# Fixed pads, shared sums stored without the residual, and a router woven into the shared experts, in a two-layer attention and mixture-of-experts kernel

## The chip, the cores and the metric

The kernel runs on one core of a Trainium2 chip. The metric is the device time of one execution in microseconds. Before the change it is 3535.88 us, the median of three runs (3523.08 to 3542.6).

## What is computed

The reference runs two layers over x, 4 sequences of 1024 tokens of width 256. A layer is an attention block and a feed-forward block, each behind a layer norm and each added to x:

```python
x = x + attn(_layernorm(x), ...)      # 16 heads of 16, causal
x = x + ffn(_layernorm(x), ...)
def ffn(x):
    shared_out = sum(relu(x @ sw1 + sb1) @ sw2 + sb2, 2 experts) / 2
    probs = softmax(x @ router_w + router_b)          # 32 experts
    topk_p, topk_i = top_k(probs, 6)                  # gates, normalised
    routed_out = sum over the experts e of gate[:, e] * (relu(x @ rw1[e] + rb1[e]) @ rw2[e] + rb2[e])
    return shared_out + routed_out
```

The first layer's attention has a distance penalty in its scores, the second's has not; both use the same feed-forward weights. Everything is float32; products are made from a high part and a rest (three matmuls for one).

## The kernel before, in words

Each engine has its own program, written out by hand, and the engines meet at semaphores. A layer has five phases, and `phase_end` between them is a barrier: every engine drains, adds to `s_phase` and waits until all five have done so.

- Phase 0 makes q, k and v for all tokens.
- Phase 1 is attention, in 16 units (`NU`) of four heads of one sequence. The router's work on a batch (a sequence) that has been through attention is spread over the four units after it (`route_step`): merge and output projection (`merge_batch`), layer norm of the rows (`normalise_rows`), their transposes and high and rest parts (`router_input`, which SP then stores to `xT_scratch` with `store_xT`), `logits`, `select` (the six largest), `place_rows` (a row number in `expert_rows` for each token and expert). POOL then scatters the rows to their experts: `dispatch(b)` is 48 indirect DMAs of 128 rows of 1280 bytes. In phase 1 this is done for batches 0, 1 and 2. Batch 2's `select` and `place_rows` come in the very last unit.
- Phase 2 is the same router chain for batch 3 (the last, `B - 1`), and after it the shared experts over 8 blocks (`NBLK`) of 512 tokens. A block is three chunks (`NCS`): `hidden` (PE, six matmuls of 512 columns) into PSUM, relu on ACT, `hidden_split` on DVE, `summed` (PE, six more), then a copy on ACT (`copy_out`), transposes back (`transpose_shared`) and on DVE `out_add`, which adds the block to the rows of x that SP loaded from `expert_sum0` into `xs32`; SP stores it back there. SP also loads the blocks' inputs (`load_shared_xT`, 1 MB each into two buffers), and the routed experts' raw weights `w2raw` and `w1raw`, which phase 3 needs. Between two blocks SP runs `close_regions` for four experts: it reads the end of an expert's rows from `prow` and writes 384 pad rows (480 KB, DRAM to DRAM) behind them, with `L545`. `expert_rows` has a fixed region for each of the 32 experts, so that a tile that runs past the expert's last row finds pads.
- Phase 3 runs the routed experts over 96 tiles of 384 rows. A table made in phase 2 (`tile_table`) gives each tile its expert and its first row. Results are added to `expert_sum0` and `expert_sum1` in turn by indirect DMA. `expert_sum1` was filled with zeros (4 MB) at the start of phase 1.
- Phase 4 adds the two sums into x.

SP's queue of DMAs is in order: what it issues later lies behind what it issued before on the same rings, and a wait of SP holds up all that is written behind it. POOL has a queue of its own.

Of the kernel before, what the change touches and what calls it, by code (L numbers as in the profile page):

```python
# [20 lines left out]
F32 = mybir.dt.float32  # L21
# [39 lines left out]
EARLY = 11  # L61
# [100 lines left out]
def build(nc, a, out):  # L162
# [6 lines left out]
    acc = [nc.dram_tensor(f"expert_sum{i}", (NTOK + TT, D), F32, kind="Internal").ap() for i in range(2)]  # L169
    tabd = nc.dram_tensor("tile_table_scratch", (P, 2), U32, kind="Internal").ap()  # L170
# [4 lines left out]
    with ctx:  # L175
# [38 lines left out]
        rowb = x[:, 4096:6656].rearrange("p (r t w) -> p r t w", r=2, t=TPB)  # L214
# [9 lines left out]
        posu = x[:, 7672:7736].bitcast(U32)  # L224
# [18 lines left out]
        table = work[:, 4032:5069]  # L243
        lincl, thr, tau, tau_rows = (table[:, i:j] for _, i, j in columns(TABLE))
        tmp = work[:, 5072:6096]
        xs32 = work[:, 6144:8192].rearrange("p (r t) -> p r t", r=2)
        raw = work[:, 8192:9728].rearrange("p (r n) -> p r n", r=3)
        ysb = work[:, 9728:10752].rearrange("p (f t) -> p f t", f=KD)
        hbuf = work[:, 10752:12288].rearrange("p (r t) -> p r t", r=3)
# [21 lines left out]
        cnt, m_e, c_e, st_e, le_e, in_e = (osb[:, NE * i:NE * i + NE] for i in range(6))  # L271
        tabf = osb[:, 192:194]
# [4 lines left out]
        tab2, prow = route_u[:, 0:2], route_u[:, 2:2 + NE]  # L277
# [33 lines left out]
        s_raw = [sem(f"shared_raw_loaded{r}") for r in range(3)]  # L311
# [7 lines left out]
        s_pad, s_zb, s_tc = sem("pad_rows_stored"), sem("second_sum_cleared"), sem("table_constants_loaded")  # L319
        s_xsl = [sem(f"shared_xT_loaded{r}") for r in range(2)]  # L320
        s_ysl = [sem(f"shared_x_loaded{r}") for r in range(2)]
        s_yss = [sem(f"shared_x_stored{r}") for r in range(2)]
# [38 lines left out]
        def _(sp):  # L361
# [9 lines left out]
            sp.dma_start(w2d, a["w2r"]).then_inc(s_init, 16)  # L371
            sp.dma_start(rows[0:TT], a["pads"]).then_inc(s_init, 16)
# [4 lines left out]
            with sp.Fori(0, NL) as L:  # L377
# [87 lines left out]

                load_values(0, 0)
# [6 lines left out]
                for u in range(NU):  # L473
# [76 lines left out]
                for blk in range(2):  # L550
                    load_shared_xT(blk)
# [1308 lines left out]
```

## Time and profile before

| | |
|---|---|
| median of three runs | 3535.88 us (3523.08 to 3542.6) |
| the profiled execution, its own time | 3527.31 us |
| span in its profile | 3525.2 us |
| PE busy | 2749.4 us, 78% |
| DVE busy | 2095.4 us, 59% |
| ACT busy, POOL busy | 1516.8 us, 1506.2 us |
| DMA | 540.23 MB, mean 153 GB/s |
| mean granted TensorE clock | 0.893 |

The span runs from the first to the last instruction; the execution's own time is 2.1 us longer. Busy time counts no waits. The shares are means over phases of very different kinds, so the stretches around phase 2 are read apart. PE is the matmul engine, DVE the vector engine, ACT the scalar engine, POOL the engine that issues indirect DMAs, SP the one that issues plain ones.

### The profile page before, as it was taken

To read this page: it belongs to the slowest core of one execution; us is meant where nothing else is said; L and a number is where in the kernel's file an instruction comes from. 1 tells how busy PE (TensorE), PEld (TensorE's weight loads), DVE (VectorE), ACT (ScalarE), POOL (GpSimd) and SP (SyncE) were. 2 spreads that over 40 slices of the span, in tenths; PEclk is the share of its full clock that TensorE was granted. 3 is DMA by queue.
4 is the path that set the end of the run, shared out by engine and by line. 5 is a ranking of instruction groups with operands and counts; after the bars stand their busy time and mean duration, and the time that the engine had idled before them with its cause. 6 is when DMAs were issued, how large, how long until landed. Compare 5 with 4: busy or idle time off the path is not lost. (4 is left out here: it accounts for less than half of the span.)

```text
span 3525.2 us, 67642 instructions
## 1 busy us (share of the span) xinstructions
PE 2749.4 (78%) x17576; PEld 2050.3 (58%) x17576; DVE 2095.4 (59%) x4312; ACT 1516.8 (43%) x2406; POOL 1506.2 (43%) x1118
## 2 busy tenths in 40 slices
PE   4789999998255999888285999999953669899880
PEld 3555555554144888787263555555522558888770
DVE  5665677764242767666375666767623337766662
ACT  2244444444011666666241454444430126666660
POOL 1520005050450688888445000222232518888882
PEclk9899999999577999999687999999975779999995
DMA  7974445451587788888668734555327768888886
GB/s 240 254 146 82 72 83 155 82 156 52 187 292 259 150 157 154 151 150 150 145 204 174 160 66 74 115 122 113 100 82 227 281 224 156 152 150 147 150 146 167
DMA packets 329916, 540.23 MB, mean 153 GB/s; under 512 B 49690, under 2 KB 246172, under 8 KB 324444
## 3 DMA queue, kind: packets, MB, share of 16 engines
q1 hardware_dynamic: 228332, 399.18, 43.2%
q0 software_dynamic: 101376, 138.47, 22.3%
q8 instruction: 106, 1.74, 0.2%
q14 instruction: 102, 0.84, 0.1%
HBM read 301.60 MB, written 283.67 MB: 166 GB/s over the span
## 5 line engine op out<-in xcount | busy, mean ns | idle before, releaser
L1390 POOL DMA_INDIRECT expert_sum<-x,route_u x576 | 950.4, 1650 | 218.4 <-issue 125.0
L1357 POOL DMA_INDIRECT expert_rows<-x x384 | 375.4, 978 | 1304.6 <-DVE x L928 1190.0
L1206 ACT ACTIVATE work<-ps 128x1024 f32<-128x1024 f32 (+3 forms) x768 | 593.9, 810 | 726.1 <-PE ps L1490 529.9
L774 DVE TENSOR_REDUCE small<-ps 128x1 f32<-128x512 f32 (+3 forms) x1216 | 726.9, 656 | 207.6 <-PE ps L1476 141.0
L1472 PE MATMUL ps<-split 128*128 128x512 f32 (+3 forms) x1536 | 512.4, 410 | 81.5 <-SPq L355 43.7
L1762 PE MATMUL ps<-split 97*128 97x256 f32 x3456 | 466.8, 291 | 86.2 <-ACT x L1287 85.6
L1486 PE MATMUL ps<-split 128*128 128x512 f32 (+3 forms) x1536 | 499.7, 405 | 18.6 <-DMA split<-split 17.6
L1762 PEld LDWEIGHTS ps<-split 97*128 97x128 f32 x3456 | 447.2, 197 | 114.8 <-issue 111.9
L1744 PE MATMUL ps<-split 128*88 128x384 f32 x2304 | 456.0, 347 | 0.4 <-DVE split L1089 0.2
L1472 PEld LDWEIGHTS ps<-split 128*128 128x128 f32 x1536 | 278.3, 202 | 274.4 <-DVE small L774 141.2
L1744 PEld LDWEIGHTS ps<-split 128*88 128x88 f32 x2304 | 352.6, 157 | 40.9 <-issue 0.8
L1287 ACT ACTIVATE x<-ps,osb 128x256 f32<-128x256 f32 x576 | 231.6, 471 | 300.3 <-DMA expert_sum<-x,route_u 292.8
L1486 PEld LDWEIGHTS ps<-split 128*128 128x128 f32 x1536 | 299.6, 201 | 77.9 <-ACT work L1206 42.4
L1503 PE MATMUL ps<-work,split 128*32 128x512 f32 (+3 forms) x3072 | 328.4, 503 | 0.0
L1109 DVE TENSOR_TENSOR split<-x,split 88x768 fp32r<-88x768 f32 x192 | 183.1, 954 | 101.2 <-ACT split L1274 99.4
L1490 PE MATMUL ps<-maskk,identb 128*128 128x128 bf16 x1024 | 233.2, 235 | 0.0
L1269 ACT ACTIVATE x<-ps,osb 88x384 f32<-88x384 f32 x384 | 209.8, 583 | 42.7 <-PE ps L1744 39.3
L1732 PE MATMUL ps<-ident,x 128*128 128x128 f32 x1152 | 168.5, 285 | 70.8 <-DMA osb<-in_b1r 39.1
L1089 DVE TENSOR_TENSOR split<-ps,split 128x768 fp32r<-128x768 f32 x192 | 182.9, 952 | 49.7 <-ACT split L1258 49.5
L1476 PE MATMUL ps<-maskq,identb 128*128 128x128 bf16 (+2 forms) x704 | 188.6, 268 | 0.0
L1258 ACT ACTIVATE split<-ps 128x768 fp32r<-128x768 f32 x192 | 157.2, 819 | 68.6 <-PE ps L1732 68.4
L1732 PEld LDWEIGHTS ps<-ident,x 128*128 128x128 f32 x1152 | 134.9, 147 | 85.0 <-issue 84.0
(170 smaller groups left out, 2926.6 us busy)
## 6 DMA issues: line engine op xcount, KB each, us to landing
x<-expert_rows SPq DMA_DIRECT2D x192, 480.0 KB
split<-qks_scratch SPq DMA_DIRECT2D x192, 256.0 KB
qks_scratch<-split SPq DMA_DIRECT2D x64, 512.0 KB, 4.5
expert_rows<-in_pads SPq DMA_DIRECT2D x65, 480.0 KB, 5.2
v_scratch<-work SPq DMA_DIRECT2D x64, 256.0 KB, 4.3
split<-v_scratch SPq DMA_DIRECT2D x32, 512.0 KB, 14.2
xT_scratch<-split SPq DMA_DIRECT2D x16, 1024.0 KB, 13.9
split<-xT_scratch SPq DMA_DIRECT2D x16, 1024.0 KB, 8.5
```

The lines of the kernel that those rows point to most:

```text
L774: v.tensor_reduce(cols[:, heads[0]:heads[0] + len(heads), i], ps[:, task_bank(n), 0:w * len(heads)].rearrange("p (h k) -> p h k", k=w), AX ...
L1206: c.activation(pexp[:, (s % 2) * 2 + h, :, BLK - w:], ps[:, 2 * h:2 * h + 2, BLK - w:], ACT.Exp).then_inc(s_pe, 1)
L1287: c.activation(ye[:, r3, k, :], ps[:, 4 + k, 0:D], ACT.Copy, scale=gsel[:, j, k:k + 1]).then_inc(s_tev, 1)
L1357: pool.indirect_dma_start(rows, bass.IndirectOffsetOnAxis(ap=posu[:, t * 8 + k:t * 8 + k + 1], axis=0), rowb[:, t // TPB, t % TPB, :], Non ...
L1390: pool.indirect_dma_start(acc[r], bass.IndirectOffsetOnAxis(ap=idx[:, j, k:k + 1], axis=0), ye[:, r3, k, :], None, compute_op=ALU.add).the ...
L1472: last = mm(bank[:, e, :], stack[:, r, 0, h, i * P:i * P + P], stack[:, r, 1, h, first:first + w], start=e == 0, stop=not diagonal and e = ...
L1486: last = mm(ps[:, h, BLK - w:], stack[:, r, 1, h, kb * P:kb * P + P], stack[:, r, 0, h, (qt + 1) * BLK - w:(qt + 1) * BLK], start=True, st ...
L1490: last = mm(ps[:, h, BLK - w:BLK - w + P], identb[:, :], maskk[:, :], start=False, stop=True, skip_group_check=True)
L1503: last = mm(ps[32 * h:32 * h + 32, 6, BLK - w:], vreg[:, r, kb, h, :], pexp[:, (s % 2) * 2 + h // 2, h % 2, BLK - w:], start=kb == 0, stop ...
L1732: last = tr(ps[:, k, n * P:n * P + P], xrow[:, r3, n, k * P:k * P + P], ident[:, :])
L1744: last = mm(ps[0:HC, 2 + c, 0:TT], w1e[:, r, ws, k * HID + c * HC:k * HID + c * HC + HC], xe[:, r, xp, k * TT:k * TT + TT], start=e == 0 a ...
L1762: last = mm(ps[:, 4 + n, 0:D], he[0:HB, r, xp, c * TT + n * P:c * TT + n * P + P], w2e[0:HB, r3, ws, c * D:c * D + D], start=e == 0 and c ...
```

## The change

It has five parts.

1. Pads. The 384 pad rows of an expert lie in front of its rows, at a fixed address. SP writes them during phase 1, two experts in each unit. Rows start 384 further on (`base`), and the tiles of an expert are counted back from the end of its rows (`rend`), so its last tile reaches into the pads. `close_regions`, which needed the counts, is gone.
2. Shared sums. `out_copy` writes a block's result without the rows of x, and SP stores it to `expert_sum1`. The filling with zeros and the loads into `xs32` are gone; the residual stays in `expert_sum0`.
3. Shared weights come as one load from a copy in DRAM that is made at the start of the kernel (0.79 MB), in the last unit of phase 1, into the place of a stack that is free by then. Their high parts (DVE) and rests (POOL) are made in that unit too. 13 experts of `w2raw`, 10 of `w1raw` and the inputs of blocks 0 and 1 are loaded in phase 1; the other 19 of `w2raw` and 22 of `w1raw` stay in phase 2, those of `w1raw` behind the last scatter (7) and the last stores (15).
4. In phase 2 the router chain of batch 3 and the shared experts are woven into each other on PE, DVE and ACT: block 0's hidden products first, then merge, and so on.
5. `dispatch(B - 2)` moves from phase 1 to phase 2, ahead of `dispatch(B - 1)`, which has its own `rowb` and `posu` buffers.

```diff
+            sp.dma_start(wsd, a["wsh"]).then_inc(s_init, 16)
...
                     if u == 0:
-                        sp.wait_ge(s_init, 64)
-                        sp.dma_start(acc[1][0:NTOK].rearrange("(t p) d -> p t d", p=P),
-                                     a["zeros"].unsqueeze(1).broadcast_to([P, NT, D])).then_inc(s_zb, 16)
+                        sp.wait_ge(s_init, 80)
                         sp.wait_ge(s_bod, (L + 1) * NT)
                         sp.dma_start(xd.rearrange("(t p) d -> p t d", p=P), xv).then_inc(s_xst, 16)
+                    for e in range(2 * u, 2 * u + 2):
+                        sp.dma_start(rows[REG0 + e * STRIDE:REG0 + e * STRIDE + TT], a["pads"]).then_inc(s_pad, 16)
...
+                    if u == 12:
+                        load_w1(0, EARLY)
+                sp.wait_ge(s_pv, (L * NU + NU - 3) * NS + NS + 2)
+                apart(sp)
+                sp.dma_start(raw.rearrange("p r n -> p (r n)"), wsd).then_inc(s_raw, 16)
                 sp.dma_start(b1, a["b1"]).then_inc(s_shared, 16)
+                load_w2(16, 24)
+                load_w2(27, 32)
...
-                for blk in range(NBLK):
-                    close_regions(4 * blk, 4 * blk + 4)
-                    if blk < NBLK - 2:
-                        load_shared_xT(blk + 2)
-                    store_shared_x(blk)
-                    if blk < NBLK - 2:
-                        load_shared_x(blk + 2)
-                load_w1(EARLY, NE)
+                for blk in range(4, NBLK):
+                    store_shared(blk)
+                load_w2(24, 27)
                 for r in range(2):
                     sp.wait_ge(s_disp[r], (L + 1) * (NBLK // 2 * TPB * TOPK * 16))
                     apart(sp)
+                load_w1(EARLY, 17)
+                for r in range(2):
                     sp.wait_ge(s_yss[r], (L + 1) * (NBLK // 2 * 16))
                     apart(sp)
+                load_w1(17, NE)
...
-                for b in range(B - 1):
+                for b in range(B - 2):
                     dispatch(b)
-                phase_end(pool, L, 1)
...
+                phase_end(pool, L, 1)
+
+
+                dispatch(B - 2)
                 dispatch(B - 1)
...
+                for c in range(NCS):
+                    hidden(0, c)
+                for r in range(2):
+                    merge_transpose(B - 1, r)
...
+                shared_part(0, 0)
+                shared_part(0, 1)
+                router_input(B - 1, 0)
+                shared_part(0, 2)
+                logits(B - 1, 0)
+                router_input(B - 1, 1)
+                shared_part(1, 0)
+                logits(B - 1, 1)
+                shared_part(1, 1)
+                shared_part(1, 2)
+                ranks(B - 1)
+                shared_part(2, 0)
...
                 merge_batch(B - 1)
                 for c in range(NCS):
-                    weights_hi(c)
-                dve.wait_ge(s_shared, (L + 1) * 16)
-                v.tensor_scalar(b1h, b1, 1.0 / NSH, None, ALU.mult).then_inc(s_b1h, 1)
+                    hidden_split(0, c)
                 batch_scales(B - 1)
                 for r in range(2):
                     normalise_rows(B - 1, r)
-                    router_input(B - 1, r)
-                    logits(B - 1, r)
+                router_input(B - 1, 0)
+                shared_step(0)
+                logits(B - 1, 0)
+                router_input(B - 1, 1)
+                logits(B - 1, 1)
                 shift_logits(B - 1)
+                out_copy(0, 0)
                 select(B - 1)
+                for c in range(NCS):
+                    hidden_split(2, c)
+                out_copy(0, 1)
                 place_rows(B - 1)
```

`shared_part(k, c)` on PE is `hidden(k + 1, c)`, `summed(k, c)` and, for c < 2, `transpose_shared(k - 1, c)`; `shared_step(k)` on DVE is `hidden_split(k + 1, c)` and `out_copy(k - 1, c)`.

On POOL, before, batch 2's 48 scatters stand ahead of the barrier that ends phase 1 (L356):

```order
L1357 DMA expert_rows<-x 144512x320 x48
L356 ISA
L1367 ISA
L1368 TENSOR_TENSOR split<-work,split 128x2x128
L1370 TENSOR_TENSOR split<-work,split 128x256
```

With the change, the rests of the shared weights stand there, and both late batches' scatters follow the barrier (L358):

```order
L1381 TENSOR_TENSOR split<-split 128x256
L358 ISA
L1367 REGISTER_ALU
L1371 DMA expert_rows<-x 144512x320 x48
L1371 DMA expert_rows<-work,x 144512x320 x48
L358 ISA
```

48 scatters have moved from before the barrier to behind it. On PE, before, phase 2 begins behind the barrier (L356) with the merge of batch 3 (L1535 transposes, L1548 products):

```order
L356 REGISTER_ALU
L1529 REGISTER_ALU
L1463 REGISTER_ALU
L1535 MATMUL ps<-ident,work 128x128 x4
L1463 REGISTER_ALU
L1535 MATMUL ps<-ident,work 128x128 x8
L1463 REGISTER_ALU
L1535 MATMUL ps<-ident,work 128x128 x4
L1542 REGISTER_ALU
L1548 MATMUL ps<-x 128x256 x4
```

With the change it begins with block 0's hidden products (L1674), and the same merge (now L1550) comes behind them:

```order
L1709 ISA
L1709 REGISTER_ALU x2
L1669 REGISTER_ALU
L1670 ISA
L1674 MATMUL ps<-split 128x512 x6
L1670 REGISTER_ALU
L1674 MATMUL ps<-split 128x512 x6
L1670 REGISTER_ALU
L1674 MATMUL ps<-split 128x512 x6
L1544 REGISTER_ALU
L1478 REGISTER_ALU
L1550 MATMUL ps<-ident,work 128x128 x4
```

18 matmuls have moved ahead of the router chain. On SP, before, the first rows of phase 2 behind the table's load are two block inputs, then a part of w2 (from `w2_scratch`), the residual rows' store (L459) and loads (L524), and the store of the transposed rows (L464):

```order
L510 DMA work<-in_table 128x1037
L548 ISA
L517 DMA split<-xT_scratch 128x2048 x2
L539 DMA split<-w_scratch 112x8x512
L455 REGISTER_ALU
L459 DMA expert_sum<-x 128x4x256 x2
L554 REGISTER_ALU
L524 DMA work<-expert_sum 128x4x256 x2
L539 DMA split<-w_scratch 112x8x512
L462 REGISTER_ALU
L464 DMA xT_scratch<-split 128x2048
```

With the change two parts of w2 (L474) come first, then the input of block 2 (L482), the residual's store (L462), block 3's input and only then the transposed rows' store (L467), behind a wait for block 1's products:

```order
L537 DMA work<-in_table 128x1037
L474 DMA split<-w_scratch 112x8x512 x2
L480 ISA
L482 DMA split<-xT_scratch 128x2048
L458 REGISTER_ALU
L462 DMA expert_sum<-x 128x4x256 x2
L480 ISA
L482 DMA split<-xT_scratch 128x2048
L465 REGISTER_ALU
L467 DMA xT_scratch<-split 128x2048
```

The loads of the residual are gone, and the store of the transposed rows has two more megabyte loads ahead of it.

## Rows read from the trace of the kernel before

**Rows 1.** The page's groups: line, engine, operation, busy us, mean ns, idle before
```profile
L1357 POOL DMA_INDIRECT expert_rows<-x x384 | 375.4, 978 | 1304.6 <-DVE x L928 1190.0
```
**Rows 2.** Windows: start:end, length, busy of each engine, clock, DMA share, GB/s
```profile
core 0: us, PE busy (x) PEld busy (x) DVE busy (x) ACT busy (x) POOL busy (x), PEclk, DMA share, GB/s
867.20:934.70 67.50, 0.00 (x0) 0.00 (x0) 3.21 (x19) 0.00 (x0) 46.10 (x48) 0.52 0.32 117
934.70:1147.60 212.90, 117.40 (x475) 96.31 (x475) 75.66 (x190) 28.99 (x44) 56.84 (x56) 0.72 0.83 278
2669.00:2882.90 213.90, 116.98 (x474) 95.60 (x474) 75.86 (x190) 28.99 (x44) 56.93 (x56) 0.72 0.83 276
```
**Rows 3.** Timeline of POOL, layer 1: start, us, what [idle before <- released by]
```profile
870.21 0.95 POOL L1357 DMA_INDIRECT expert_rows<-x  x1 [104.30 <-DVE x L928]
...
929.66 0.96 POOL L1357 DMA_INDIRECT expert_rows<-x  x1 [0.30 <-issue]
...
993.52 0.98 POOL L1357 DMA_INDIRECT expert_rows<-x  x1 [38.72 <-DVE x L928]
...
1055.45 0.96 POOL L1357 DMA_INDIRECT expert_rows<-x  x1 [0.30 <-issue]
```
**Rows 4.** Timeline of PE around phase 2, layer 1, and layer 2's start
```profile
935.10 3.65 PE L1535 MATMUL ps<-ident,work 128*128 128x128 f32 x16 [67.93 <-POOLq L355]
...
994.40 7.03 PE L1674 MATMUL ps<-split 128*128 128x512 f32 x18 [0.45 <-issue]
...
1020.16 2.90 PE L1674 MATMUL ps<-split 128*128 128x512 f32 x6 [8.30 <-DMA split<-xT_scratch]
...
1026.18 1.52 PE L1685 MATMUL ps<-split 128*128 128x512 f32 x6
1027.54 1.53 PE L1674 MATMUL ps<-split 128*128 128x512 f32 x6
...
1040.26 2.90 PE L1674 MATMUL ps<-split 128*128 128x512 f32 x6 [8.93 <-DMA split<-xT_scratch]
...
1147.59 1.51 PE L1732 MATMUL ps<-ident,x 128*128 128x128 f32 x6 [19.68 <-DMA osb<-in_b1r]
...
2669.36 3.55 PE L1535 MATMUL ps<-ident,work 128*128 128x128 f32 x16 [68.28 <-POOLq L355]
```
**Rows 5.** Timeline of SP in phase 2, layer 1: DMA issues
```profile
961.40 0.34 SPq L464 DMA_DIRECT2D xT_scratch<-split  x1
...
1124.47 5.50 SPq L545 DMA_DIRECT2D expert_rows<-in_pads  x4
...
1130.76 0.50 SPq L535 DMA_DIRECT2D work<-in_w1r  x1
```
**Rows 6.** Timeline of DVE, end of phase 1 and in phase 2, layer 1
```profile
855.13 0.26 DVE L799 RECIPROCAL small<-ps 128x16 f32<-128x16 f32 x1 [11.51 <-PE ps L1513]
...
870.52 0.42 DVE L802 TENSOR_TENSOR work<-ps,small 128x256 f32<-128x256 f32 x1
...
972.25 0.69 DVE L856 CAST split<-ps 128x512 fp32r<-128x512 f32 x1 [3.90 <-DMA xT_scratch<-split]
...
1024.01 0.43 DVE L1019 CAST split<-work 128x512 fp32r<-128x512 f32 x1 [11.42 <-ACT work L1241]
1024.48 0.69 DVE L1021 TENSOR_TENSOR split<-work,split 128x512 fp32r<-128x512 f32 x1
```
**Rows 7.** Timeline of PE, first units of phase 1: layer 1, layer 2
```profile
273.33 0.79 PE L1486 MATMUL ps<-split 128*128 128x512 f32 x1 [4.49 <-DMA split<-split]
...
2008.92 0.50 PE L1486 MATMUL ps<-split 128*128 128x512 f32 x1 [3.06 <-DMA split<-split]
```
**Rows 8.** DMA issues by line: count, KB each, median us from issue to landing
```profile
expert_rows<-in_pads SPq DMA_DIRECT2D x65, 480.0 KB, 5.2
...
split<-xT_scratch SPq DMA_DIRECT2D x16, 1024.0 KB, 8.5
...
expert_sum<-work SPq DMA_DIRECT2D x16, 512.0 KB, 6.1
...
w_scratch<-in_w2r SPq DMA_DIRECT2D x1, 26.5
```

More of the change, by code:

```diff
@@ L60 @@
 W2ROWS = 112
-EARLY = 11
+EARLY = 10
 UPB = T // BLK
@@ L310, in build @@
                                    sem("selection_counted"))
-        s_raw = [sem(f"shared_raw_loaded{r}") for r in range(3)]
+        s_raw = sem("shared_raw_loaded")
         s_wh, s_wl = sem("shared_hi_done"), sem("shared_lo_done")
@@ L538, in load_w2 @@
-                def load_w2(first, last):
-                    sp.dma_start(w2raw[:, first * W2:last * W2].rearrange("p (e n) -> p e n", n=W2),
-                                 w2d[first:last].rearrange("e p n -> p e n")).then_inc(s_wr2, 16)
-                def close_regions(first, last):
-                    with sp.Fori(first, last) as e:
-                        at = sp.value_load(prow[0:1, ds(e, 1)], min_val=REG0, max_val=NROWS - TT)
-                        sp.dma_start(rows[ds(at, TT), :], a["pads"]).then_inc(s_pad, 16)
+                    if u == 12:
+                        load_w1(0, EARLY)
@@ L1699, in transpose_shared, with shared_part @@
                     last.then_inc(s_yt, 1)
-                def shared_block(blk):
-                    for c in range(NCS):
-                        hidden(blk, c)
-                        if blk and c == 2:
-                            transpose_shared(blk - 1, 0)
-                        if c >= 2:
-                            summed(blk, c - 2)
-                        elif blk:
-                            summed(blk - 1, c + 1)
-                        if blk and c == 2:
-                            transpose_shared(blk - 1, 1)
+                def shared_part(k, c):
+                    if k < NBLK - 1:
+                        hidden(k + 1, c)
+                    summed(k, c)
+                    if k and c < 2:
+                        transpose_shared(k - 1, c)
                 for c in range(NCS):
                     pe.wait_ge(s_wl, L * NCS + c + 1)
-                for blk in range(NBLK):
-                    shared_block(blk)
+                for c in range(NCS):
+                    hidden(0, c)
+                for r in range(2):
+                    merge_transpose(B - 1, r)
+                for r in range(2):
+                    for h in range(2):
+                        merge_product(B - 1, r, h)
+                shared_part(0, 0)
[10 more added lines that the diff above has]
+                shared_part(2, 0)
+                pe.wait_ge(s_ms, (L + 1) * B)
+                task_free(route_task(B - 1, 15))
+                apart(pe)
+                mm(ps[:, task_bank(route_task(B - 1, 15)), 0:NE], oneb[:, :], msumb, start=True,
+                   stop=True).then_inc(s_mj, 1)
                 for c in (1, 2):
-                    summed(NBLK - 1, c)
+                    shared_part(2, c)
+                for k in range(3, NBLK):
+                    for c in range(NCS):
+                        shared_part(k, c)
                 for f in range(2):
```

230 lines of the change are left out of this document (114 added, 116 removed).

## The prediction

> **What bounds the kernel now.** I read the page's groups first, then the windows of the stretches in which PE idles, then the timelines of POOL, PE, SP and DVE there. The page shows that POOL's scatters of rows (384 in two layers, mean 978 ns) have little idle time between them once they run: what they cost is decided by when they may start [rows 1]. The windows show two bad stretches in each layer. Between 867.20 and 934.70 PE does nothing at all and POOL is the only engine with work [rows 2]: the reader is to see that batch 2's scatters begin at 870.21, when DVE has just placed the rows, that the last begins at 929.66, and that PE's next matmul at 935.10 waited 67.93 us for POOL's share of the barrier [rows 3, 4]. Layer 2 has the same, 68.28 us [rows 4]. The second stretch is phase 2, from there to phase 3's first transpose at 1147.59, 212.5 us. PE is busy 117.4 of the window's 212.9 at a granted clock of 0.72 (a mix of the levels 1.2 and 2.4 GHz), while the DMA engines are busy 83% at 278 GB/s [rows 2, 4]. In it the router chain of batch 3 comes first, alone, until its first scatter at 993.52; then the shared blocks, which begin 20.1 us apart (1020.16, 1040.26), each behind an 8 to 9 us wait for its input [rows 3, 4]. POOL is done with the last scatter at 1056.4; it is not the bound of phase 2, SP's queue is: four pads (1.97 MB) stand ahead of each block's input, and the last four hold SP from 1124.47 to 1130 and the loading of w1 behind them, for which phase 3 waits [rows 3, 5].
>
> **Batch 2's scatters out of phase 1.** DVE's last work in phase 1 ends at 870.52 + 0.42 = 870.9 [rows 6]. From the last scatter's end (930.6) to PE's first matmul (935.1) the barrier takes 4.5 us, with POOL's queue just emptied; without that I take 2 (bounds 0.5 and 4.5). So phase 2 starts at 873 and not at 935.1: 62 us a layer (60 to 64). What comes into the last unit instead is hidden: DVE's six casts of the shared weights stand where it idled 11.5 us before 855.13 [rows 6], and POOL's rests lie beside the attention. If the load they need were late, all of it would come back; it is issued one unit ahead, so I charge nothing (up to 3).
>
> **Phase 2, counted from its first matmul.** The new order [the two lists of PE] makes one chain, then a scatter, then a tail.
> - *Until batch 3's rows are placed.* Before it takes 993.52 - 935.10 = 58.4 us [rows 3, 4]. Put into it are 18 hidden products at the head, 7.0 us at the low clock as at 994.40 [rows 4], and on DVE three blocks' splits, 9 pairs of 1.16 us (0.47 to the second instruction, then 0.69), 10.4 us [rows 4, 6]. The weight casts leave. PE's other products fall largely beside DVE's work, and with PE busy the router's own matmuls should run nearer the full clock: the first six products after a wait take 2.90 us, those in a run 1.53 [rows 4]. The store of the transposed rows, for which DVE already waits 3.9 us at 972.25 [rows 6], now has a block's input ahead of it (8.5 us [rows 8]); I charge 5. Sum 58.4 + 7 + 10.4 + 5 = 80.8, less some 10 for the overlap and the clock: 70 (bounds 60 and 90).
> - *Scatters.* Batch 2's need 870.21 to 930.6, 60.4 us, alone; batch 3's needed 993.52 to 1056.4, 62.9 us, beside DVE [rows 3]. The queue is free at 62, rows are there at 70, the last scatter ends at 133 and has landed at 135.
> - *PE.* At 70 blocks 0 and 1 and part of 2 are done. A block at full clock is six groups of six products, 1.36 us from one to the next (1026.18 to 1027.54 [rows 4]), with transposes about 9.2 us; five and a half more give 50, a stall of 5 for the count of rows, the last copies 3, so 128, and the last store lands 6.1 us later [rows 8] at 134. POOL and PE end together: either is cover for the other, and if one is late the phase is.
> - *Tail.* w1 is issued when both have landed, at 135. Before, 21 experts' load of 3.7 MB from 1130.76 released phase 3 at 1147.59, 16.8 us later, with pads and a store still ahead in the queue [rows 4, 5]. Now 22 experts without them: 17. Phase 3 begins at 152 instead of 212.5: 60.5 us a layer.
>
> **DMA.** The window moved 278 GB/s x 212.9 us = 59.2 MB [rows 2]. Out go 32 pads (15.7 MB, 480 KB each [rows 8]), the residual's loads (4.2), 13 experts of w2 (3.0), two block inputs (2.1), 1.8 of w1 and 0.8 of raw weights; in come 48 scatters of 128 x 1280 bytes (7.9). That leaves 39.5 MB, 260 GB/s over 152 us, below the 278 that the stretch held at a share of 83%. At 278 it would need 142 us. So the queue isn't the bound, but not far from it; that is my reason for 5 us on the store above.
>
> A rule speaks against the new scatters. The row: beside DVE's work 48 scatters took 62.9 us, alone 60.4, so DVE costs them 2.5 us, with some ten split pairs inside [rows 3]. The Trainium skill (SBUF — State Buffer, the part on the engine ports and the trap in which DVE blocks DMA) says that a float32 copy on DVE locks GpSimd, which writes the descriptors, out of the shared port for the whole instruction. By the rule in full all 24 pairs would be added to the scatters, as the second rival has it, and the execution would take 3339. By the row it is 2.4 times 2.5 us over both batches, 6 us, of which only batch 3's share is on the path. I go by the row.
>
> **Phase 1 and the start.** Two pads a unit are 0.98 MB, issued early in the unit; they are through long before the next rows of maxima. The zeros' 4 MB are gone from the first unit, where PE waited 4.49 us (273.33) and 3.06 us (2008.92) for its rows of maxima behind them [rows 7]: -5 of the 7.6. At the start of the kernel the copy of the shared weights (0.79 MB) joins a queue in which the 3.67 MB of w2 take 26.5 us [rows 8] and in front of the first weights: 26.5 x 0.79 / 3.67 = 5.7 at most, +4. Phases 3 and 4 have the same tiles and additions: nothing.
>
> **Sum** against the profiled execution's own time: 3527.3 - 2 x (62 + 60.5) - 5 + 4 = 3281. That execution is 8.6 us under the median of 3535.9; half of that is added: 3285.
>
> **The rivals.**
> - *Phase 2 stays bound by DMA* (0.14). For it: 83% busy now, a second batch's scatters come in, and six block inputs still wait for a buffer. Against it: the pads, ahead of every input, are gone. If each block from 70 on shows its input's whole 8.5 us [rows 8] beside its 9.2 of matmuls, six take 106, so 176, the store lands at 182, phase 3 begins at 199: 13.5 saved there instead of 60.5, 3285 + 94 = 3379.
> - *The scatters starve beside DVE*, the lock above as this kernel would have it (0.07): 24 pairs x (0.43 + 0.69) us [rows 6] = 27 us a layer on POOL's chain. For it: 2.5 us show. Against it: only these. 3285 + 54 = 3339. The rule is the Trainium skill's, named above.
> - *The wait has only moved* (0.02): batch 2's 60.4 us push batch 3's scatters and with them the end by as much; no gain from that part, and 3536 if phase 2's own gain goes with it. Against it: 91 us pass between the last scatter's end and phase 3's first transpose, and batch 3's rows aren't placed before 58.4 anyway [rows 3, 4].
> - *Slower* (0.03): pads ahead of the rows of maxima. Each unit but the first of a layer starts when these 16 KB have landed, and they use the pads' queue. If a pair of pads (5.2 us each [rows 8]) lay ahead each time, 30 units x 10.4 = 312 us are lost against 246 gained: 3600. It decides from 8.2 us a unit. The pads are issued right behind a unit's load, the rows late in the next, so I expect both to be through by then; the two waits of [rows 7] show the mechanism, with 8 MB ahead.
>
> The forecast itself has 0.74, with a range of its own of 3250 to 3325: rows placed at 60, where POOL's queue is the bound (127 instead of 135 for the landing), and all of the zeros' wait back, give 3285 - 16 - 3 = 3266; a barrier of 0.5 us and a head of 4 instead of 7 make it 3255; rows at 90 give 3285 + 40 = 3325. The range for 8 in 10 takes in the starving scatters: 3245 to 3340. A measurement can tell 0.5% (18 us) from no change: faster 0.96, same 0.01, slower 0.03.
>
> **What the profile after would show.** PE's idle time in front of phase 2 is 6 us, not 68. Batch 2's scatters start within 3 us of the barrier, batch 3's about 70 us after it; 48 take 61 to 64. Shared blocks from the third on begin 9 to 11 us apart, with waits for inputs under 2 us. Phase 3's first transpose comes 145 to 160 us after phase 2's first matmul. The wait of 4.49 us in phase 1 is gone, and the first weights' split is 2 to 6 us later. It would be wrong if blocks still wait 5 us or more for their input, if batch 3's rows come at 90 or later, or if waits for the rows of maxima appear in the units of phase 1.

## The result and the profile after

In the text TensorE, VectorE or DVE, ScalarE, GpSimd and SyncE are the engines that the rows call PE, DVE, ACT, POOL and SP.

The changed kernel took 3251.9 us (median of 4 runs, 3248.9 to 3254.4), the kernel before 3539.2 beside it on the same chip; the ratio is 0.9196 with a 95% interval of 0.9165 to 0.9226. On a second chip it was 3245.5 us and 0.9200 (0.9178 to 0.9221). The forecast was 3285, with a range of 3245 to 3340. The profiled execution took 3251.45 us, 275.9 less than the profiled one of before; the sum had it at 3281. The time lies in the range, 33 us under the forecast and 7 us above the range's lower end; on the second chip it is above that end by 0.5 us.

TensorE's rows at the same places as in [rows 4], from the timeline after:

```profile
877.69 2.90 PE L1674 MATMUL ps<-split 128*128 128x512 f32 x6 [4.54 <-DVEq L357]
...
941.71 0.19 PE L1732 MATMUL ps<-x,oneb 128*128 128x32 bf16 x1 [2.79 <-DVE x L931]
...
961.66 1.52 PE L1674 MATMUL ps<-split 128*128 128x512 f32 x6
...
970.79 1.52 PE L1674 MATMUL ps<-split 128*128 128x512 f32 x6
...
979.91 1.52 PE L1674 MATMUL ps<-split 128*128 128x512 f32 x6
...
996.82 0.63 PE L1697 MATMUL ps<-ident,work 128*128 128x128 f32 x4 [0.88 <-DVE work L1034]
...
1020.47 1.51 PE L1752 MATMUL ps<-ident,x 128*128 128x128 f32 x6 [23.02 <-DMA osb<-in_b1r]
...
2471.69 6.98 PE L1674 MATMUL ps<-split 128*128 128x512 f32 x18 [4.54 <-DVEq L357]
...
2613.30 1.51 PE L1752 MATMUL ps<-ident,x 128*128 128x128 f32 x6 [23.54 <-DMA osb<-in_b1r]
```

Ahead of phase 2 TensorE idles 4.54 us instead of 67.93 and 68.28. Phase 2, from the first matmul to phase 3's first transpose, is 142.8 us in layer 1 and 141.6 in layer 2, where it was 212.5 and 213.6. The late blocks start 9.1 us apart, and no wait for `xT_scratch` is left among them. The row at 941.71 is the product that counts each expert's rows; TensorE waited 2.79 us for it. Its last transposes of the shared blocks end 119.8 us into the phase, and the last copy of a sum on DVE 120.5 us into it.

GpSimd's scatters (as [rows 3]) and SyncE's last issues (as [rows 5]), same layer:

```profile
877.91 0.98 POOL L1371 DMA_INDIRECT expert_rows<-x  x1 [10.98 <-DVEq L357]
...
941.46 0.95 POOL L1371 DMA_INDIRECT expert_rows<-work,x  x1 [1.62 <-DVE work L921]
...
1002.23 0.96 POOL L1371 DMA_INDIRECT expert_rows<-work,x  x1 [0.30 <-issue]
```
```profile
983.29 15.34 SPq L545 DMA_DIRECT2D expert_sum<-work  x4
998.68 0.57 SPq L474 DMA_DIRECT2D split<-w_scratch  x1
1006.30 0.98 SPq L470 DMA_DIRECT2D work<-in_w1r  x2
```

Batch 2's 48 scatters begin right behind the barrier and batch 3's follow with a gap of 1.62 us. The last ends at 1003.2, 125.5 us into the phase; SyncE issues w1 at 1006.3, when it has landed, and phase 3 follows 14.2 us later. So the chain that sets the end of phase 2 is now GpSimd's two runs of scatters, the second of which begins when batch 3's rows are placed; TensorE ends 6 us before it. The router's one long wait on DVE in the phase, to be read against 972.25 in [rows 6], is for the store of the transposed rows, 6.26 us:

```profile
918.37 0.69 DVE L849 CAST split<-ps 128x512 fp32r<-128x512 f32 x1 [6.26 <-DMA xT_scratch<-split]
```

The windows of the phase, to be read against [rows 2]:

```profile
core 0: us, PE busy (x) PEld busy (x) DVE busy (x) ACT busy (x) POOL busy (x), PEclk, DMA share, GB/s
877.69:1020.47 142.78, 103.87 (x474) 84.74 (x475) 70.08 (x183) 28.77 (x44) 99.05 (x98) 0.83 0.81 275
2471.69:2613.30 141.61, 102.42 (x475) 83.66 (x475) 70.62 (x183) 28.80 (x44) 99.83 (x98) 0.84 0.82 276
```

TensorE's same work takes 14 us less there, at a granted clock of 0.83 instead of 0.72. By stage the 275.9 us go: the start and layer 1's phase 0 +3.5, its phase 1 and the barrier -60.9, its phase 2 -69.7, its phases 3 and 4 -5.0; then layer 2 in the same order +1.2, -66.8, -72.0 and -6.2.

### The profile page after: what moved, and what is told of

The parts are those of the page before. It is cut to its first block and busy times, and to the rows that moved or that the text cites. A ratio compares the mean times of both kernels' runs of the same rounds, so it can differ in the third digit from the quotient of the medians.

```text
span 3249.4 us, 67087 instructions
## 1 busy us (share of the span) xinstructions
PE 2719.4 (84%) x17576; PEld 2022.0 (62%) x17576; DVE 2096.4 (65%) x4312; ACT 1517.0 (47%) x2406; POOL 1497.5 (46%) x1118
## 5 line engine op out<-in xcount | busy, mean ns | idle before, releaser
L1405 POOL DMA_INDIRECT expert_sum<-x,route_u x576 | 940.1, 1632 | 213.3 <-issue 119.4
L1371 POOL DMA_INDIRECT expert_rows<-x x288 | 280.7, 975 | 1010.0 <-DVE x L921 902.3
## 6 DMA issues: line engine op xcount, KB each, us to landing
split<-v_scratch SPq DMA_DIRECT2D x32, 512.0 KB, 14.2
```

The costliest lines, as they stand in the source:

```text
L1371: pool.indirect_dma_start(rows, bass.IndirectOffsetOnAxis(ap=posu[b][:, t * 8 + k:t * 8 + k + 1], axis=0), rowb[b][:, t // TPB, t % TPB, : ...
L1405: pool.indirect_dma_start(acc[r], bass.IndirectOffsetOnAxis(ap=idx[:, j, k:k + 1], axis=0), ye[:, r3, k, :], None, compute_op=ALU.add).the ...
```

## The experiments

Each ran beside the kernel before on the same chip; "phase 2" is layer 1's and layer 2's length from its first matmul to phase 3's first transpose, read from TensorE's timeline of the profiled execution. It is not the same twice: the eight phases of kernels whose code for it is the changed kernel's (this one, its repetition and the two below that only change phase 1) are 139.0 to 143.7 us long.

**One part undone: batch 2's scatters early again.**

```diff
+                dispatch(B - 2)
                 phase_end(pool, L, 1)
-                dispatch(B - 2)
                 dispatch(B - 1)
```


> The changed kernel with one part undone: batch 2's 48 scatters are issued before the barrier that ends phase 1, as in the kernel before. Theory (POOL's chain bounds both places): TensorE again stands idle 64 to 68 us ahead of phase 2 (4.5 in the changed kernel), and phase 2 stays close to its 142 us, since batch 3's scatters begin at row placing (about 62 us into it) anyway: 3252 + 2 x 63 = about 3378 (3370 to 3390). Rival (the late scatters slowed phase 2, by POOL and DVE sharing a port or by DMA traffic): phase 2 falls to 130 to 136 us, and the time is 3352 to 3366.

3372.5 us, ratio 0.9558 (0.9525 to 0.9591). The idle time is back, and the phase is nearly unchanged, 139.3 and 139.8 us, though 48 scatters fewer run in it:

```profile
938.32 2.04 PE L1674 MATMUL ps<-split 128*128 128x512 f32 x4 [68.20 <-POOLq L357]
...
1077.61 1.51 PE L1752 MATMUL ps<-ident,x 128*128 128x128 f32 x6 [23.74 <-DMA osb<-in_b1r]
```
```profile
938.32:1077.61 139.29, 101.47 (x475) 83.04 (x475) 69.36 (x183) 28.80 (x44) 51.51 (x50) 0.84 0.71 225
```

The theory holds. The moved scatters gain 63 us a layer. What they cost in phase 2, 2 to 4 us against the changed kernel's profile, is inside the spread of 139.0 to 143.7, so no cost is shown. DMA carries 225 GB/s here and 275 in the changed kernel, for nearly the same length, so the bytes don't set that length.

**The kernel before with late scatters alone.** `dispatch(B - 2)` behind the barrier, batch 3's rows in `work[:, 1440:4000]`, early w1 only for 4 experts:

```diff
-EARLY = 11
+EARLY = 4
-                for b in range(B - 1):
+                for b in range(B - 2):
                     dispatch(b)
                 phase_end(pool, L, 1)
 ...
+                dispatch(B - 2)
                 dispatch(B - 1)
```


> The kernel before with one part of the change alone: batch 2's scatters after the barrier (with rows of their own for batch 3, in room taken from the early w1 loads, so 28 instead of 21 experts' w1 are loaded behind the last scatter). Theory (phase 2 of the kernel before, 212 us, is bound by SP's queue of pads and block inputs, so 62 us more of POOL's scatters fit beside it): TensorE's 68 us idle ahead of phase 2 falls to 4 to 6, phase 2 stays at 212 to 220: 3535 - 2 x 60 = about 3415 (3405 to 3430). Rival (DMA-bound phase 2): the moved scatters' traffic lengthens phase 2 by 15 to 60 us, and the time is 3440 to 3535.

3410.9 us, 0.968 (0.9639 to 0.9722), as the theory has it. The idle time fell to 4.31 and 4.22 us, phase 2 grew to 222.8 and 222.3, 2 to 3 us more than the theory's 220. Of these 9 to 10 us some 3 are the longer load of w1 behind the last scatter (TensorE's last wait is 22.65 us, [rows 4] has 19.68). Another 5 to 6 are longer waits for the blocks' inputs, of which this is the first: 46.2 and 46.5 us in the two layers, 41.2 and 40.3 before.

```profile
872.88 3.65 PE L1538 MATMUL ps<-ident,work 128*128 128x128 f32 x16 [4.31 <-DVEq L356]
...
962.92 2.90 PE L1677 MATMUL ps<-split 128*128 128x512 f32 x6 [8.60 <-DMA split<-xT_scratch]
```

The DMA engines moved 301 GB/s in this phase 2, so the 278 of [rows 2] were not the most that they can do there.

**The kernel before with fixed pads in phase 1 alone.** Cut to SyncE's lines:

```diff
+                    for e in range(2 * u, 2 * u + 2):
+                        sp.dma_start(rows[REG0 + e * STRIDE:REG0 + e * STRIDE + TT], a["pads"]).then_inc(s_pad, 16)
 ...
-                    close_regions(4 * blk, 4 * blk + 4)
```


> The kernel before with one part of the change alone: pads fixed in front of each expert's rows, stored in phase 1 (two per unit). Theory (the pads in SP's queue made phase 2 212 us): without them the queue ends early, POOL's 48 scatters of batch 3 end at 58 + 63 = 121 us or TensorE's blocks after the router chain at 130 to 140, and phase 3 begins 145 to 160 us after phase 2's first matmul: -55 to -67 us a layer, 3400 to 3430; the 68 us idle ahead of phase 2 stays. Rival (residual loads, stores and scatters hold it as much): phase 2 stays over 180 us, and the time is over 3470. If the 5 to 6 us of phases 3 and 4 come from pads in front, they show here too.

3443.4 us, 0.9749 (0.9704 to 0.9795), between the two. Phase 2 fell to 169.8 and 170.0, 43 us less and not 55 to 67. Its scatters end 123.8 us into the phase, but the shared blocks, which start only behind the router chain, go on until 154:

```profile
1007.26 0.98 POOL L1359 DMA_INDIRECT expert_rows<-x  x1 [40.89 <-DVE x L930]
```
```profile
1008.14 6.30 PE L1676 MATMUL ps<-split 128*128 128x512 f32 x18 [0.45 <-issue]
...
1099.10 0.63 PE L1699 MATMUL ps<-ident,work 128*128 128x128 f32 x4 [0.88 <-DVE work L1031]
...
1115.86 1.51 PE L1734 MATMUL ps<-ident,x 128*128 128x128 f32 x6 [16.13 <-DMA osb<-in_b1r]
```

So with the pads gone the next bound is TensorE's order of work, which the other parts of the change move. Phase 1 grew by 8 to 10 us a layer: with the zero filling still there, TensorE's waits for rows of maxima are 6.54 and 6.38 us, where [rows 7] has 4.49 and 3.06, and layer 1 drew the long copy told of below. In layer 2, where the kernel before has the long copy too, that wait is 3.3 of the 7.9 us; the rest is left open.

**The kernel before with fixed pads where they were,** so that only the address is a constant (cut to SyncE's lines):

```diff
-                    with sp.Fori(first, last) as e:
-                        at = sp.value_load(prow[0:1, ds(e, 1)], min_val=REG0, max_val=NROWS - TT)
-                        sp.dma_start(rows[ds(at, TT), :], a["pads"]).then_inc(s_pad, 16)
+                    for e in range(first, last):
+                        sp.dma_start(rows[REG0 + e * STRIDE:REG0 + e * STRIDE + TT], a["pads"]).then_inc(s_pad, 16)
```


> The kernel before with pads fixed in front of each expert's rows, but stored where they were, four ahead of each shared block's input in phase 2: only the address, read from VectorE's numbers before, becomes a constant. In the kernel before four pads kept SP's queue 6.3 to 6.8 us, fixed ones 2.6 to 2.7. Theory (the issue time in SP's queue is what the pads cost phase 2): the eight groups take 8 x 4 = 32 us less, phase 2 is about 180 us instead of 212: 3526 - 2 x 32 = 3462 (3450 to 3475). Rival (the pads' bytes, or the waits of stores and residual loads in the queue, set the pace): phase 2 stays at 205 to 213: 3512 to 3530.

3489.7 us, 0.989 (0.9863 to 0.9916), between the theory and the rival. Four pads hold the queue 2.4 us, but phase 2 is 194.0 and 200.3, 18.4 and 13.3 us less and not 32 each: half of what the theory has.

```profile
1041.30 2.45 SPq L545 DMA_DIRECT2D expert_rows<-in_pads  x4
1043.95 0.73 SPq L518 DMA_DIRECT2D split<-xT_scratch  x1
1050.82 0.36 SPq L532 DMA_DIRECT2D expert_sum<-work  x1
1058.17 0.36 SPq L525 DMA_DIRECT2D work<-expert_sum  x1
```
```profile
936.94:1130.98 194.04, 117.48 (x474) 96.05 (x475) 75.78 (x190) 28.69 (x44) 55.98 (x56) 0.74 0.88 304
```

The window moves 59.0 MB at 304 GB/s, before 59.2 at 278 [rows 2]. The first blocks are still 17 to 18 us apart (before: 20.1): input, store and residual wait on one another, and the pads lie between them. Of the 43 us that go when the pads leave phase 2, 13 to 18 go with the read address alone; the rest goes only when the stores leave the phase.

**The changed kernel with the pads back in phase 2.** Fixed, four ahead of each block's input as before:

```diff
-                    for e in range(2 * u, 2 * u + 2):
-                        sp.dma_start(rows[REG0 + e * STRIDE:REG0 + e * STRIDE + TT], a["pads"]).then_inc(s_pad, 16)
 ...
+                pad_regions(12, 16)
                 load_shared_xT(6)
                 store_shared(2)
+                pad_regions(16, 20)
                 load_shared_xT(7)
```


> The changed kernel with the fixed pads stored in phase 2 instead of phase 1: 32 stores of 5 us each in SP's queue, four ahead of each block's input from the third block on. Theory (what held phase 2 before was the pads in the queue of the blocks' inputs): 166 us of pads in the queue push the last shared block to 170 to 190 us after phase 2's first matmul, TensorE waits for xT inputs again (over 10 us a block), phase 3 begins 190 to 205 us after it: +50 to +60 us a layer, 3350 to 3375. Rival (fixed pads need no wait, so they run beside the rest and POOL's chain of 125 us still ends last): phase 2 stays within 5 us of 142 and the time is 3245 to 3265.

3279.6 us, 0.9297 (0.9272 to 0.9321). Both missed. Phase 2 is 156.3 and 157.5 us, 14 to 16 more. TensorE's idle time in it is 13 to 14 us longer, from two sides. Waits for inputs are back in part, 5.5 us in layer 1 and 7.2 in layer 2. Waits for DVE's copies of sums are 10.7 and 9.0 us where the changed kernel has 2.4. The latter come from the tile table's way through memory, behind which SyncE's stores of the sums queue, then DVE, then TensorE:

```profile
972.17 2.24 PE L1684 MATMUL ps<-split 128*128 128x512 f32 x6 [3.26 <-DMA split<-xT_scratch]
...
985.37 1.86 PE L1684 MATMUL ps<-split 128*128 128x512 f32 x6 [2.23 <-DMA split<-xT_scratch]
...
1012.14 1.09 PE L1707 MATMUL ps<-ident,work 128*128 128x128 f32 x4 [7.11 <-DVE work L1044]
```
```profile
968.59 4.14 SPq L548 DMA_DIRECT2D expert_rows<-in_pads  x4
972.85 0.52 SPq L574 DMA_DIRECT2D tile_table_scratch<-route_u  x1
997.15 0.25 SPq L577 DMA_DIRECT2D osb<-tile_table_scratch  x1
997.60 0.38 SPq L543 DMA_DIRECT2D expert_sum<-work  x1
```
```profile
1011.30 0.69 DVE L1044 COPY work<-ps 128x512 f32<-128x512 f32 x1 [8.28 <-DMA expert_sum<-work]
```

That store of the table takes 24.3 us to be waited for, against 12.2 in the changed kernel. My 166 us were 32 pads times the time from issue to landing [rows 8]. In a queue that takes four fixed pads in 2.45 us (the run above) and in 4.14 here, this is latency, not a price each.

**The changed kernel without turns.** Router first, then the eight blocks, and SyncE stores the transposed rows ahead of the blocks' inputs again; cut to DVE's lines:

```diff
-                for c in range(NCS):
-                    hidden_split(0, c)
                 batch_scales(B - 1)
 ...
-                shared_step(0)
                 logits(B - 1, 0)
 ...
-                shared_step(3)
                 tile_table_rows()
-                for k in range(4, NBLK):
+                for k in range(NBLK):
                     shared_step(k)
```


> The changed kernel with the last batch's router first and then the eight shared blocks, in the order of the kernel before, instead of in turns. Theory (POOL's two runs of 48 scatters, 62 us each, bound phase 2; turns only keep TensorE's end under that): batch 3's rows are placed 8 to 12 us earlier, but POOL's queue is free only at 62 us, so the last scatter ends as before at 125; TensorE's blocks begin at about 58 and end at 132 to 136, which makes it the bound by 8 to 12 us: phase 2 is 150 to 155 us, +8 to +14 a layer, 3268 to 3280. Rival 1 (turns are worth nothing): 3245 to 3258. Rival 2 (the turns delay the rows and so POOL): phase 2 shortens, below 3245.

3262.0 us, 0.9243 (0.9217 to 0.9269), between the theory and rival 1; the intervals of this ratio and the changed kernel's overlap, so the times alone don't decide. Phase 2 does: 148.6 and 148.4 us, 6 to 7 more than in the changed kernel's profile and above all of its 139.0 to 143.7, just under the theory's 150. The scatters end at 124.7 and 124.5, as with turns; w1 is issued at 1011.9, 131.6 us in, behind stores of sums that end later:

```profile
1000.38 10.72 SPq L545 DMA_DIRECT2D expert_sum<-work  x3
1011.16 0.50 SPq L474 DMA_DIRECT2D split<-w_scratch  x1
1011.90 2.75 SPq L470 DMA_DIRECT2D work<-in_w1r  x2
```

**The changed kernel with residual loads and zeros back.** Cut to DVE's lines:

```diff
-                    if blk >= 2 and f == 0:
-                        dve.wait_ge(s_yss[r], (L * (NBLK // 2) + blk // 2) * 16)
-                        apart(dve)
+                    dve.wait_ge(s_ysl[r], (L * (NBLK // 2) + blk // 2 + 1) * 16)
                     dve.wait_ge(s_yt, (L * NBLK + blk) * 2 + f + 1 + 1)
-                    v.tensor_copy(ysum[:, r, f * BLK:f * BLK + BLK], ps[:, 6, :]).then_inc(s_ya, 1)
+                    half = ysum[:, r, f * BLK:f * BLK + BLK]
+                    v.tensor_tensor(half, ps[:, 6, :], half, ALU.add).then_inc(s_ya, 1)
```


> The changed kernel with the plain storing of the shared experts' sums undone: x is loaded again from the first sum and added, the sum goes back there, and the second sum is filled with zeros in phase 1. Theory (this part gave only the zeros' wait of 3 to 5 us a layer in phase 1, since POOL's chain ends phase 2): phase 1's first wait of 4.5 us is back, phase 2 grows by 0 to 5 us from eight loads of 8 us in SP's queue: +3 to +10 us a layer, 3258 to 3272. Rival (the residual loads hold the blocks as the pads did): blocks wait for their x, phase 2 grows by 15 us or more: over 3280. The 5 to 6 us that phases 3 and 4 lost per layer tell where they belong: if they come from this part, those phases return to 629 and 642 us.

3275.9 us, 0.9284 (0.924 to 0.9327), above the theory's 3272 and below the rival's 3280. Phase 2 is 146.9 and 146.8 us, 4.1 and 5.2 us longer, as expected. Phase 1's wait for rows of maxima is back at 6.65 and 7.39 us, and the changed kernel, with pads and no zeros, doesn't have it. With pads in the same queue the zeros cost more than without (4.49 and 3.06 in [rows 7]).

```profile
279.45 0.79 PE L1524 MATMUL ps<-split 128*128 128x512 f32 x1 [6.65 <-DMA split<-split]
```

**GpSimd's bias additions later,** in both kernels (the reason is in the last section):

```diff
                 pool.wait_ge(s_zero[2], (L + 1) * 2)
+                pool.wait_ge(s_neg, L * NU + 1)
                 apart(pool)
                 with pool.Fori(0, NT) as t:
```


> The kernel before, but GpSimd's 32 bias additions at the start of phase 1 wait until VectorE has done its first two copies of the maxima. Theory (VectorE's small 128x16 copy can't share the port with GpSimd's additions, and takes 12 us instead of 0.8 when it falls among them, which it did in the kernel before in one layer of two and in the changed kernel in both): the copy takes under 1 us in both layers, TensorE's wait for it is 3 us in both, and the time is 10 us under the profiled 3527 and about 15 to 21 under the median 3539: 3515 to 3525, with less spread than 3523 to 3543. Rival (the long copy is a wait that the profile puts down wrongly, or the additions are needed by then): no change, 3523 to 3543.

> The changed kernel with the same one wait: GpSimd's 32 bias additions begin when VectorE's first copies of the maxima are done. Theory: both layers' copies fall from 11.9 to 0.8 us, TensorE's wait from 13.5 to 3 us, -10.5 us a layer: 3252 - 21 = 3231 (3226 to 3238). Rival: the additions, 22 us from then, make the x store or the first batch's loads late by as much, and nothing is gained: 3245 to 3255.

3522.6 us, 0.9986 (0.9967 to 1.0005), and 3242.8 us, 0.919 (0.9153 to 0.9227). The first lies in its theory's range, but the kernel before beside it took 3526.1; the second lies between its two ranges. Neither shows a gain that the runs can tell. The mechanism is there (0.17 us for the copy), the gain isn't. TensorE's waits of phase 1 in the changed kernel, then with the addition later:

```profile
199.85 0.37 PE L1536 MATMUL ps<-ident,small 128*32 128x128 f32 x1 [13.48 <-DVE small L778]
203.82 0.79 PE L1501 MATMUL ps<-split 128*128 128x512 f32 x1 [3.60 <-DMA split<-split]
```
```profile
186.49 0.27 PE L1537 MATMUL ps<-ident,small 128*32 128x128 f32 x1 [1.72 <-DVE small L778]
197.68 0.79 PE L1502 MATMUL ps<-split 128*128 128x512 f32 x1 [10.93 <-DMA split<-split]
```

The maxima are issued 13 us earlier (187.41 instead of 200.88) and land 10 us after their issue instead of 3, behind the second unit's stacks: the DMA engines are busy 92% from 185 to 190 us, and without them ahead, in the next run, the landing takes 3 us again. The long copy had hidden that. TensorE's first unit goes on 5.0 us sooner after the start of phase 1 in layer 1 and 6.5 in layer 2, of the 10.5 that were counted on, and the two together are less than a measurement tells.

**The maxima first in the queue.**

```diff
+                load_neg_max(0)
                 for r in (1, 2):
                     load_rows(r)
                     load_stack(r, r)
                     load_values(r, r)
-                    if r == 1:
-                        load_neg_max(0)
```


> The changed kernel with the bias additions after VectorE's first copies of the maxima, and the store of these maxima issued ahead of the second and third units' loads. With the first edit alone TensorE's first wait of phase 1 fell from 13.5 to 2.8 us and the next grew from 3.6 to 9.4 and 10.9 us, since the store was issued 13 us earlier, behind 24 us of loads. Theory (those loads' bytes delay it): the second wait is back at 3.6 us, the two together 6 to 7 us instead of 17: 10 to 11 us a layer less than the changed kernel, 3229 to 3236 if that is 3252. Rival (the second unit's loads, 15 us later, are then awaited): a new wait of 5 us or more at the second unit, and no more than the first edit's 9 us in all: 3240 to 3248.

3268.1 us, 0.9256 (0.924 to 0.9273), slower than the changed kernel beside it by 22.6 us and outside both ranges. The first waits are 1.7 and 3.6 us, as the theory has them, and the rival's mechanism takes back more than all of it, with a wait of 20 us where it had 5 or more: everything behind the waiting store in SyncE's queue, the second unit's loads first, starts some 20 us later (at 190.0 instead of 170.4).

```profile
191.52 0.79 PE L1501 MATMUL ps<-split 128*128 128x512 f32 x1 [3.61 <-DMA split<-split]
...
214.85 1.11 PE L1487 MATMUL ps<-split 128*128 128x128 f32 x4 [20.40 <-DMA split<-rows_scratch]
```

**And more of w1 earlier,** on top of the two edits just before:

```diff
+                for r in range(2):
+                    sp.wait_ge(s_yss[r], (L + 1) * (NBLK // 2 * 16))
+                    apart(sp)
+                load_w1(18, NE)
                 for r in range(2):
                     sp.wait_ge(s_disp[r], (L + 1) * (NBLK // 2 * TPB * TOPK * 16))
                     apart(sp)
-                load_w1(EARLY, 17)
+                load_w1(EARLY, 18)
```


> The kernel just before this one, with expert weights 18 to 31 loaded as soon as the shared sums are stored, ahead of the wait for the last scatters, and 10 to 17 behind it, instead of 10 to 16 behind the scatters and the rest last. Theory (behind the last scatter there lie 14 to 15 us: landing, 22 experts' weights, then the barrier): with 8 instead of 22 experts behind it, 2 to 4 us a layer: 4 to 8 us less than the kernel just before. Rival (TensorE and the shared sums end only 6 us before the scatters, and the first tile's load and the barrier are most of the tail): within 3 us of it.

3271.3 us, 0.9258 (0.9236 to 0.9279): the rival. Phase 2 is 140.9 us in both layers against 141.5 and 141.2. The sums have landed at 1010.3, only 3.5 us before the last scatter ends, so the load can't be brought forward by much.

**The changed kernel again,** to see what two runs of one kernel differ by:

> The changed kernel itself, beside the next two on the same chip. Theory: 3250 (3244 to 3258), with phases 3 and 4 of the first layer anywhere from 624 to 634 us, as they were in kernels that have the same ones; no reason of this study gives another value.

3245.5 us. In its profiled execution phase 2 is 139.0 and 143.7 us, at granted clocks of 0.86 and 0.82, and phases 3 and 4 of layer 1 take 630.7. The profiled executions of this study's kernels have 624.0 to 634.0 there; both ends are the changed kernel's code for these phases. In layer 2 they have 630.7 to 642.3. The 5 and 6 us that these phases seemed to gain lie within this spread, so they are no gain that a part of the change can be credited with.

## Why the prediction was right

The path was right: scatters that had stood alone fit into phase 2, and the pads in SyncE's queue had held that phase. The size was 33 us too high, and the low end of the range took the time in by 7 us (0.5 on the second chip). That end was not well founded: with rows placed early GpSimd's queue is the bound and a shorter head saves nothing, and 1.5 us of barrier and 3 us of head a layer take 3266 to 3257, not 3255.

- *Batch 2's scatters out of phase 1.* 62 us a layer (60 to 64) forecast; TensorE's idle time fell by 63.4 and 63.7, and undoing this part alone cost 3372.5 - 3248.7 (the mean of the changed kernel's two medians) = 124 us, 62 a layer.
- *Until batch 3's rows are placed.* The term that was mis-sized: 70 us forecast, 63.8 and 63.5 measured. The products at the head were right (6.98 us), the longer wait for the store was not (5 more forecast, 2.4 measured: 6.26 at 918.37 against 3.90). What is left, 58.4 + 7 + 10.4 + 2.4 - 63.8 = 14 us, was put down to the overlap and the clock, at 10; no run tells these two apart. GpSimd's queue came free at 62, as forecast, so the rows are no longer the bound by more than 1.6 us.
- *Scatters.* 61.9 and 61.7 us for 48, forecast 60.4 and 63. The last ends at 125.5, not 133. They don't starve beside DVE's copies, which were the second rival: all 24 pairs fall into the two runs of scatters, which took 1.5 and 1.3 us more in layer 1 than the 60.4 alone. The rule as the prediction quotes it speaks of the copy alone, 0.43 us of a pair, so by it 24 pairs come to 10 us a layer; the 27 also count the second instruction, which is no copy. Even the 10 don't show.
- *TensorE.* The last copy ends at 120.5 instead of 128. Counted from the placing of the rows that is 57 us where 58 were forecast: blocks of 9.1 us as forecast, and a stall for the count of 2.8 instead of 5.
- *Tail.* Forecast 17 from issue, measured 14.2. With the terms above phase 3 starts at 142.8 and 141.6 where 152 was forecast, under the 145 to 160 named as what the profile would show. Phase 2 gave 141.7 us over both layers where 121 were forecast: 20.7 of the 29.6 us by which the sum was too high. Another 11.2 are phases 3 and 4, forecast at nothing, which is spread (above). All that lies ahead of phase 2 gave 123 us over both layers, 2 less than the 125 of the sum.
- *DMA.* 39.3 MB moved, 39.5 forecast, at 275 GB/s. That this gave 142 us "at 278" was chance: with 48 scatters fewer the phase took 139.3 us at 225 GB/s. And 278 was no ceiling: the stretch held 301 and 304 GB/s in two of the runs above.
- *What bounded phase 2 before.* The pads in SyncE's queue, as said: 43 of some 70 us go with them alone. The prediction reads 20.1 us and a wait of 8 to 9 us for every block; the rows it shows are of the first two, and in layer 1 the later ones start 16 to 19 us apart with waits of 4 to 8. The parts don't add up, since each bound hides the next: undone singly, pads cost phase 2 14 to 16 us, turns 6 to 7, residual 4 to 5, against a spread of 4.7 in one and the same phase.
- *Phase 1 and the start.* Start +3.5 (forecast 4). The waits of 4.49 and 3.06 us are gone, 7.6 us where 5 was forecast. Layer 1's first unit waited 13.48 and 3.60 us, and in the profiled execution of before 2.96 and 6.46: 7.7 us lost to the long copy, which the forecast did not have. Pads never delayed the rows of maxima: the slower rival did not happen. So the long copy took back what the zeros' waits gave; whether the change makes it more likely is left open in the last section.
- *Offset to the median.* The 4 us added for it explain nothing: over four measurements the medians of the kernel before were 3524.6 to 3539.2, and the profiled 3527.3 lies within them.

## What to carry to other kernels

Before a barrier, look for an engine that works alone and whose results only the stage after next needs; moving it behind the barrier is worth its whole length as long as it doesn't lengthen that stage's longest chain, so add up each engine's chain there first. Several bounds of a stage can lie close together (phase 2 is 142 us with no part undone, 147, 148 and 157 with one): undo parts singly and do them singly, since the two give different prices. A DMA's time from issue to landing is not its price in a queue, and a store moved ahead in an in-order queue makes everything behind it wait for its data.

## What the runs showed of the hardware

DVE's small copy of the first unit's maxima (128x16 elements) takes 0.17 us in other units, but beside GpSimd's 32 additions it took 0.7 to 0.8 us in some layers and 11.9 to 12.4 in others. The kernel before has both, layer 1 and layer 2:

```profile
183.63 0.81 DVE L784 COPY small<-small 128x16 f32<-128x16 f32 x1
...
1912.62 12.01 DVE L784 COPY small<-small 128x16 f32<-128x16 f32 x1
```
```profile
174.09 21.93 POOL L1350 TENSOR_TENSOR x<-x,small 128x256 f32 x32 [0.34 <-POOL split L1344]
...
1902.71 21.89 POOL L1350 TENSOR_TENSOR x<-x,small 128x256 f32 x32 [0.34 <-POOL split L1344]
```

1912.62 + 12.01 is 1924.63, and the additions end at 1902.71 + 21.89 = 1924.60: the copy ended when GpSimd's whole train of additions was over, while the one at 183.63 was done after about one of them (0.68 us each). With the additions held back until the copies are done it takes 0.17 us in both layers. The Trainium skill (SBUF — State Buffer, the section on the two separate sides) says that the engine that starts first holds a port pair that both share for its whole instruction, and that the other is blocked. The 0.8 us agree with that. The 12 us are longer than one instruction, as if a gap between two of GpSimd's were not always enough for DVE to get in; that is an argument, no run shows the port. What decides between the two lengths was not settled. Among the kernels without that wait, layer 1 has the long copy in all five profiles of kernels without the zero filling and in one of five with it, layer 2 in nine of ten, so that the change makes it more likely in layer 1 is possible and not shown. Where the copy was short TensorE waited longer for the rows of maxima behind it, so of its 11 us it cost the first unit 5 to 8.
